# Graph network on one core: edges in four chunks, record sums beside the edge rounds, PSUM accumulation at register columns

## The chip, the cores and the metric

The kernel runs on one core of a Trainium2 chip. The time is the device time of a run in microseconds; a comparison is a median over several runs. The core has a matrix engine (PE, TensorE), a vector engine (DVE, VectorE), a scalar engine (ACT, ScalarE), GpSimd (POOL, which here issues the indirect DMAs, that is gathers and scatters with a row number per partition) and a queue engine (SP, SyncE). Each works through its own program in order and waits on semaphores for the others.

## The reference

12500 nodes with 32 features, 200000 edges sorted by destination, sources random. Everything is f32.

```python
h = relu(layernorm(x))                                   # 12500 x 32
fwd = concat(h[dst], h[src], edge_attr)                  # 200000 x 80
bwd = concat(h[src], h[dst], edge_attr)
flow = relu([fwd; bwd] @ Wf1 + bf1) @ Wf2 + bf2          # 64 wide
total = segment_sum(flow, [dst; src])                    # per node
x = x + relu(total @ Wn1 + bn1) @ Wn2 + bn2
h2 = relu(layernorm(x))
out = x + segment_sum(h2[dst], src)
```

So each edge adds a 64-wide value to its destination and another to its source, and in the second layer its destination's h2 row to its source.

## The kernel before

Nodes lie in 98 blocks of 128. Edges are worked on in tiles of 128 (one edge per partition). A tile belongs to one block of destinations, so a tile that crosses a border between blocks is worked on twice; with 1563 real tiles this makes 1664 slots, as 104 windows (NI) of 16 tiles, each window being four rounds (R) of four tiles (U). A schedule computed on the chip tells for each slot its block (`blk`), its first edge (`e0`) and its position in the ring of gathered rows (`gs_row`). It is made twice, once by destination and once by source.

**Start.** h is computed, split into three bf16 parts (`h3`), and a table `t2_rows` of 128-wide rows per node (h times the source half of Wf1) is made on PE and written to DRAM, in 26 steps. Both schedules are made.

**Edge stage.** Per round, GpSimd gathers four tiles of `t2_rows` into `ring` (L610, two rounds ahead of use) and scatters the four tiles of 67-word records of an earlier round to the place at which they lie sorted by source (L620). PE adds the gathered rows to the product of the destination's expanded features and the edge attributes (L943, L944), transposes one-hots (L914), counts how many edges of each source block came before (L955 to L959), expands destination rows (L926), and sums over destinations (L972). ScalarE evicts and applies relu (L756 to L778). VectorE computes record positions from the counts (`positions`, L1275 to L1281), adds four blocks to `acc` (L1266) and prepares the one-hots of the round after next (L1238 to L1261). SP loads source and destination numbers and the edge attributes. The scatter of a round waits for its positions and its relu.

**Record stage**, once all records have been scattered. 104 windows of 16 record slots are read back in order of source. VectorE makes one-hots u = 0 and 2 (L1337), GpSimd those of u = 1 and 3 (L654), PE multiplies each with its records into one of four banks (L1010), VectorE adds each of the four results to its block of `acc` (L1266), ScalarE copies the indices that come with the records (L802).

**Nodes.** 13 steps of the two node matrices, then the second layer norm; h2 is written to DRAM.

**Second layer.** GpSimd gathers h2 rows for each record tile (L674, 16 windows of ring), VectorE makes four one-hots per group (L1422), PE multiplies (L1072), VectorE adds four results to `xs` (L1266).

Order is as written: no scheduler moves instructions. All loops are hardware loops over windows.

Of the kernel before, what the change touches and what calls it, by code (L numbers as in the profile page):

```python
# [50 lines left out]
DA, DB, HC = 13, 8, 800  # L51
EA_PARTS = 8
H3 = 3 * D
SW = 4
TW = -(-(-(-E // P)) // W)
RING = 16
RG = 8 * W
NTW = TW
assert NI % 8 == 0 and NTW % 8 == 2 and RG >= NB - 1 + 3 * U
assert E % 125 == 0 and JC <= 512 and J % 4 == 0 and NI % SW == 0 and TW < NI - SW and EP >= TW * W * P and EP // P - W < TW * W  # L60

# [34 lines left out]
def build(nc, x, sd, ea, w12_in, w3_in, wf2e_in, wn1_in, bn1_in, wn2_in, bn2_in, out):  # L96
    with ExitStack() as ctx:
# [13 lines left out]
        by_d_sd = dram("by_d_sd", [EP, 2], I32)  # L111
        by_d_ea = dram("by_d_ea", [EA, EP])
        fb_rows = dram("fb_rows", [NP, NB])
        fb_cols = dram("fb_cols", [NP, NB])
        t2_rows = dram("t2_rows", [NBP * P, P])
        records = dram("records", [EP, REC])
# [19 lines left out]
        hprod = sb("hprod", [DA * 8, DB, 8])  # L136
        hsum = sb("hsum", [DA * 8, DB])
        hexp = sb("hexp", [DA * 8, DA, DB])
        ncol = sb("ncol", [NB, 1])
        tail_rec = sb("tail_rec", [P, REC])  # L140
        w12 = sb("w12", [P, U, P])
        w3 = sb("w3", [H3 + 1 + EA, P])
# [12 lines left out]
        ring = ring_flat.rearrange("p (t c) -> p t c", c=P)  # L155
# [3 lines left out]
        rest = ring_flat[:, 2 * LN_:RG * P]  # L159
        acc = sb("acc", [P, NBP, ACC])  # L160
        acc_flat = acc[:, :, :].rearrange("p b c -> p (b c)")
        jrow = sb("jrow", [NB, J])[:, :]

        srec = [rest[:, w * W * REC:(w + 1) * W * REC].rearrange("p (t c) -> p t c", c=REC) for w in range(SW)]
        at_ = SW * W * REC
        accs = rest[:, at_:at_ + 2 * U * ACC].rearrange("p (k u c) -> p k u c", k=2, u=U)
        at_ += 2 * U * ACC
        accT = rest[0:ACC, at_:at_ + 2 * U * P].rearrange("p (k n) -> p k n", k=2)
        at_ += 2 * U * P
        nodeT = rest[0:2 * HID, at_:at_ + U * P]  # L170
        at_ += U * P
        assert at_ <= RG * P - 2 * LN_

# [3 lines left out]
        pairs = raw[:, :, :].rearrange("p k j -> p (k j)").bitcast(F32).rearrange("p (j k) -> p j k", k=2)  # L177

        wide = sb("wide", [P, 2, J])
        wide_flat = wide[:, :, :].rearrange("p k j -> p (k j)")  # L180
# [41 lines left out]

        rec = sb("rec", [P, R, U, REC])
        rec_i = sb("rec_i", [P, R, U, 2], I32)
        sidx = sb("sidx", [P, 8, W, 2], I32)
        sdf = sb("sdf", [P, 2, U, 2])
        small = sb("small", [P, 2, 7, U])
        sblk = sb("sblk", [P, 2, U], I32)
# [1275 lines left out]
```

## Time and profile before

| | us |
|---|---|
| timed, median of 3 | 9032.03 (9025.67 to 9038.92) |
| profiled execution, first to last instruction | 7224.1 |
| start, to the first scatter | 168 |
| edge stage, to its end at | 4325 |
| record stage | 803 |
| nodes | 94 |
| second layer | 2002 |

Shares of the profiled span: PE 61%, DVE 44%, ACT 19%, GpSimd 72%. The 1808 us between the profiled span and the timed median are seen in no row of the profile. "busy" of GpSimd is the time its indirect DMAs take to issue, not the transfer. "issue" is idle time in which the engine waited for nothing that the profile shows. An f32 matmul has two records in the trace.

### The profile page before, as it was taken

What the parts mean: (1) busy time and instruction counts of PE and PEld (TensorE: products, weight loads), DVE (VectorE), ACT (ScalarE), POOL (GpSimd) and SP (SyncE); (2) the same over time, 40 slices, a digit from 0 to 9 for tenths busy, and PEclk for the clock granted to TensorE, in tenths of its full rate; (3) what the DMA queues carried; (4) which work ended last, traced back from release to release, by engine and by line L of the source; (5) the groups of instructions that cost most, each with busy time, mean ns of one, the idle gap of its engine ahead of it and who ended that gap; (6) DMA issues with size and microseconds to landing.
All of it is one profiled execution on the core that took longest, in us unless ns stands there. A gap on an engine that the chain in (4) does not pass through costs nothing.

```text
span 7224.1 us, 127054 instructions
## 1 busy us (share of the span) xinstructions
PE 4419.8 (61%) x23241; PEld 3987.8 (55%) x23244; DVE 3200.3 (44%) x15358; ACT 1352.3 (19%) x4288; POOL 5197.9 (72%) x5767
## 2 busy tenths in 40 slices
PE   4666666666666666666666679999733333333333
PEld 3655556555555655555565569999533333333333
DVE  5444444444444444444444466666523232323232
ACT  2222222222222222222222234434200000000000
POOL 2777777777777777777777766666377777777776
PEclk8666676666766666766667785555655555555555
DMA  5222222222222222222222123333111111111111
GB/s 154 43 46 43 43 43 43 43 42 43 42 43 43 42 43 42 42 42 42 43 42 42 41 35 73 71 71 73 30 14 14 14 14 14 14 14 14 14 14 20
DMA packets 1109393, 290.45 MB, mean 40 GB/s; under 512 B 992782, under 2 KB 1058701, under 8 KB 1108518
## 3 DMA queue, kind: packets, MB, share of 16 engines
q0 software_dynamic: 153824, 183.68, 10.7%
q1 hardware_dynamic: 954758, 88.54, 10.3%
q10 hardware_dynamic: 576, 16.16, 0.7%
q14 instruction: 216, 1.77, 0.1%
q8 instruction: 19, 0.31, 0.0%
HBM read 223.49 MB, written 82.32 MB: 42 GB/s over the span
## 4 chain that ended last, share of the span: by engine, by line
POOL 59%; issue 27%; DVE 6%; PE 3%; DVEq 2%; DMA 2%; POOLq 0%; ACT 0%; ACTq 0%; SPq 0%
POOL records L620 21%; POOL ring L674 20%; POOL ring L610 18%; DVE acc L1266 3%; DVEq L331 1%; PE bank L1010 1%; DVE oht L1337 1%; DVE ohd L1337 1%; DVEq L1266 1%; DMA ring<-records 0%; PE bank L943 0%; PE bank L846 0%; DMA row_next<-in_sd 0%; PE bank L944 0%; PE bank L972 0%
## 5 line engine op out<-in xcount | busy, mean ns | idle before, releaser
L620 POOL DMA_INDIRECT records<-rec,pos x1664 | 1650.3, 992 | 526.7 <-issue 507.8
L674 POOL DMA_INDIRECT ring<-h_rows,didx x1568 | 1491.1, 951 | 576.3 <-issue 477.5
L610 POOL DMA_INDIRECT ring<-t_rows,sidx x1568 | 1519.5, 969 | 484.9 <-issue 482.1
L943 PE MATMUL bank<-ring,ident 128*128 x3328 | 1094.3, 431 | 1254.6 <-DMA ring<-t_rows,sidx 1249.8
L943 PEld LDWEIGHTS bank<-ring,ident 128*128 128x128 f32 x3328 | 868.4, 320 | 1309.9 <-issue 1309.8
L1072 PE MATMUL bank<-ring,ohd 128*128 x1664 | 376.2, 402 | 1282.8 <-POOLq L684 1282.2
L1072 PEld LDWEIGHTS bank<-ring,ohd 128*128 128x128 f32 x1664 | 362.9, 330 | 1295.9 <-issue 1295.9
L1275 DVE TENSOR_TENSOR prod<-bank,q_row 128x392 f32<-128x392 f32 x416 | 235.7, 567 | 1895.8 <-PE bank L959 1895.6
L944 PE MATMUL bank<-w,cmb 113*128 113x128 f32 x3328 | 1026.2, 411 | 0.0
L1266 DVE TENSOR_TENSOR acc<-acc,bank 128x65 f32 x3328 | 734.6, 221 | 524.9 <-issue 279.1
L1266 DVE TENSOR_TENSOR xs<-xs,bank 128x32 f32 x1664 | 304.3, 183 | 1384.2 <-PE bank L1072 1371.3
L944 PEld LDWEIGHTS bank<-w,cmb 113*128 113x128 f32 x3328 | 883.0, 324 | 0.0
L773 ACT ACTIVATE rf<-bank 128x256 f32<-128x256 f32 x416 | 159.8, 384 | 2735.3 <-PE bank L944 2733.2
L972 PE MATMUL bank<-rf,ohd 128*128 128x65 f32 x3328 | 453.1, 279 | 9.7 <-ACT rec L778 0.3
L972 PEld LDWEIGHTS bank<-rf,ohd 128*128 128x128 f32 x3328 | 407.9, 193 | 54.4 <-issue 3.1
L1010 PE MATMUL bank<-ring,ohd 128*128 x1664 | 381.7, 421 | 62.4 <-POOL ohd L654 62.0
L1010 PEld LDWEIGHTS bank<-ring,ohd 128*128 128x128 f32 x1664 | 362.9, 330 | 80.7 <-issue 80.7
L802 ACT CAST raw<-ring (+1 forms) x1664 | 312.4, 192 | 478.6 <-DMA ring<-records 337.5
L1010 PE MATMUL bank<-ring,oht 128*128 x1664 | 382.3, 418 | 6.4 <-issue 6.4
L1010 PEld LDWEIGHTS bank<-ring,oht 128*128 128x128 f32 x1664 | 369.2, 332 | 10.7 <-issue 10.6
L1072 PE MATMUL bank<-ring,oht 128*128 x1664 | 374.5, 401 | 0.0
L1072 PEld LDWEIGHTS bank<-ring,oht 128*128 128x128 f32 x1664 | 367.4, 333 | 0.0
(213 smaller groups left out, 6508.9 us busy)
## 6 DMA issues: line engine op xcount, KB each, us to landing
ring<-records SPq DMA_DIRECT2D x104, 536.0 KB, 4.3
rec_i<-by_d_sd SPq DMA_DIRECT2D x1664, 1.0 KB
cmb<-by_d_ea SPq DMA_DIRECT2D x1664, 8.0 KB
records<-rec,pos POOLq DMA_INDIRECT x1664
ring<-t_rows,sidx POOLq DMA_INDIRECT x1568
ring<-h_rows,didx POOLq DMA_INDIRECT x1568, 2.4
by_d_ea<-in_ea ACTq DMA_DIRECT2D x8, 1579.0 KB, 19.1
t_rows<-cmb SPq DMA_DIRECT2D x26, 256.0 KB, 2.2
```

Source lines behind the costliest of these rows:

```text
L610: nc.gpsimd.indirect_dma_start(out=ring[:, m * W + r * U + u, :], out_offset=None, in_=t2_rows, in_offset=bass.IndirectOffsetOnAxis(ap=sid ...
L620: nc.gpsimd.indirect_dma_start(out=records, out_offset=bass.IndirectOffsetOnAxis(ap=pos[:, r, u:u + 1].bitcast(U32), axis=0), in_=rec[:, r ...
L674: nc.gpsimd.indirect_dma_start(out=h2g[:, w * W + t, :], out_offset=None, in_=h2_rows, in_offset=bass.IndirectOffsetOnAxis(ap=didx[:, k, t ...
L773: nc.scalar.activation(rf[:, :, 0:HID], pre[:, :, 0:HID], ACT.Relu)
L802: ins = nc.scalar.copy(pairs[:, bass.ds(j0 + u, 1), :].rearrange("p a k -> p (a k)"), srec[w][:, bass.ds(at[u], 1), HID + 1:REC].bitcast(I ...
L943: nc.tensor.matmul(p, ident[:, :], ring[:, bass.ds(at[u], 1), :].rearrange("p a c -> p (a c)"), start=True, stop=False)
L944: ins = nc.tensor.matmul(p, cmb[:, r, u, :], w3[:, :], start=False, stop=True)
L972: ins = nc.tensor.matmul(pb[3][:, u * ACC:(u + 1) * ACC], ohd[:, r % 2, u, :], rf[:, u, :], start=True, stop=True)
L1010: ins = nc.tensor.matmul(s_bank[r][:, u * ACC:(u + 1) * ACC], s_oh[r][:, u, :], srec[w][:, bass.ds(at[r * U + u], 1), 0:ACC].rearrange("p ...
L1072: ins = nc.tensor.matmul(s_bank[r][:, u * D:(u + 1) * D], s_oh[r][:, u, :], h2g[:, bass.ds(at[r * U + u], 1), :].rearrange("p a f -> p (a ...
L1266: return nc.vector.tensor_tensor(to, to, src[:, u * width:(u + 1) * width], ALU.add)
L1275: placed = chain.link(nc.vector.tensor_tensor(prod[:, :, :], q[:, 0:U, :], bcast_mid(q_row[:, r % 2, :], U), ALU.add))
```

## The change

1. **Edges and records in chunks.** The edge tiles are divided into four chunks of 480, 400, 336 and 347 tiles. Records are sorted by source within their chunk. A chunk's records are complete once its edges are through, so they can be summed while the next chunk's edges are worked on. Record windows are now of 24 slots (`SWIN`), six groups (`SG`) of four; there are 84 of them (`NS`), 2016 slots instead of 1664. The record position's base per chunk comes in through one more matmul in `counts` (a row of offsets chosen by a register).
2. **Sums beside the edges.** From edge window 40 (`I0`) on, each edge window also sums one record window: two groups in rounds 0 and 2, one in rounds 1 and 3 (`PLAN`). PE does `sum_records`, VectorE `sum_step`, which adds a group's four results one by one and makes all four one-hots of the group after; ScalarE keeps two index columns per window for the second layer (`keep_columns`). GpSimd makes no one-hots any more. 64 windows are summed so.
3. **The other 20 windows** (120 groups) come after the edges, in `add_up_records`: a one-row matmul clears 260 columns, the four products are accumulated at columns that depend on the slot's block (same block as its predecessor or the next), and VectorE adds all four blocks in one instruction of 260 columns.
4. **The second layer** sums in the same way, 504 groups with one add of 128 columns each; its gathers are written out without a loop and take their indices from the kept columns.
5. **Gathers of the edge stage** fetch 96 bf16 numbers (the three parts of h) instead of 128 f32 numbers; the table steps at the start are gone. PE transposes the gathered rows (`transpose_sources`), ScalarE evicts them, and the product with the source weights joins the one with the attributes. A product with the destination weights takes the place of the product with the identity. Gathers lead by four rounds (`LEAD`), and scatters stand ahead of gathers.
6. **Source and destination numbers** are loaded once into SBUF; ScalarE picks them per tile (`pick_edges`) instead of four loads per round on SP.
7. The **source schedule** is made after the first edge window instead of before it.

```diff
+PLAN = (2, 1, 2, 1)
+CHUNKS = (480, 400, 336, -(-E // P) - 1216)
+SR = 2
+I0 = 40
...
-            def gather_t2(s, m, r):
+            def gather_h3(s, m, r):
...
+            def sum_records(s, m):
+
+                n = s * SG + m
+                at = four(pe, slot_row, n * U, SR * SWIN - 1)
+                pe.wait_ge(soh_ready, n + 1)
+                pe.sem_inc(pe_tick, 1)
+                for u in range(U):
+                    ins = nc.tensor.matmul(e_bank[m % 2][:, u * ACC:(u + 1) * ACC], e_oh[m % 2][:, u, :],
+                                           srec[:, bass.ds(at[u], 1), 0:ACC].rearrange("p a c -> p (a c)"), start=True, stop=True)
+                ins.then_inc(ssum_ready, 1)
+
+            def add_up_records(s, m):
...
+                nc.tensor.matmul(e_bank[m % 2][:, 0:U * ACC], ones_h[0:1, :], before_h[0:1, 0:1].broadcast_to([1, U * ACC]), start=True, stop=False)
+                for u in range(U):
+                    ins = nc.tensor.matmul(e_bank[m % 2][:, block_columns(to, u, ACC)], e_oh[m % 2][:, u, :],
+                                           srec[:, bass.ds(at[u], 1), 0:ACC].rearrange("p a c -> p (a c)"), start=False, stop=u == U - 1)
+                ins.then_inc(ssum_ready, 1)
...
+            def sum_step(s, m, adds=True, ahead=True, behind=None):
...
+                for u in range(U):
+                    if adds:
+                        dve.wait_ge(dve_s, DS0 + (n - 1) * U + u)
+                        ins = add_step(acc, at, e_bank[(m - 1) % 2], ACC, u)
+                        ins.then_inc(dve_s, 1)
+                    if ahead:
+                        record_one_hot(s1, m1, at1, u)
...
+                    m = sum(PLAN[:r + 1]) - 1
+                    if s is not None and PLAN[r] == 2:
+                        sum_step(s, m - 1, adds=not (start and m == 1), behind=i * R + r)
+                    add_and_prepare(i, r, first, ahead, None if s is None or start and r == 0 else (s * SG + m - 1) * U)
+                    if s is not None:
+                        sum_step(s, m, behind=i * R + r + 1)
```

VectorE, from the end of a round's positions to its first add to `acc`. Before (`TENSOR_LOAD sched` reads the blocks of four slots into registers, `ISA` is a wait or a register step):

```order
L1280 TENSOR_REDUCE small<-prod 128x4
L1281 TENSOR_TENSOR pos<-small 128x4
L325 TENSOR_LOAD sched
L1266 ISA
L1266 TENSOR_TENSOR acc<-acc,bank 128x65
L1238 CAST sdf<-rec_i 128x8
```

After, in a round with two record groups:

```order
L1388 TENSOR_TENSOR pos<-small 128x4
L364 ISA
L364 TENSOR_LOAD sched
L364 ISA
L364 TENSOR_LOAD sched
L1454 REGISTER_ALU
L1373 ISA
L1373 TENSOR_TENSOR acc<-acc,bank 128x65
L1432 ISA
L1432 REGISTER_ALU
L1432 TENSOR_SCALAR oht<-iota,wide,ring 128x128
L1454 REGISTER_ALU
```

Two register loads and four pairs of add and one-hot have come between the positions and the edges' own adds; the same stands once more behind those adds.

TensorE, between the counts and the sums of a round. Before (`sched` is the destination block, `h` is `h3`):

```order
L959 MATMUL bank<-ohs,ones_h 128x98
L325 ISA
L325 TENSOR_LOAD sched
L926 ISA
L926 MATMUL bank<-oht,h 96x128
```

After, in a round with two record groups (`ring` is the records' ring, the one-hots lie in `ring` or `oht`):

```order
L979 MATMUL bank<-ohs,ones_h 128x98
L364 ISA
L364 TENSOR_LOAD sched
L999 REGISTER_ALU
L1002 ISA
L1002 MATMUL bank<-ring 128x65
L1002 ISA
L1002 MATMUL bank<-ring 128x65
```

A group's four matmuls stand ahead of the expansion; the second group's stand behind the round's sums (L992), ahead of the next round's hidden layer.

GpSimd, in the loop over windows. Before:

```order
L610 DMA ring<-t_rows,sidx 128x128 x4
L615 ISA
L620 DMA records<-rec,pos 202112x67 x4
L610 DMA ring<-t_rows,sidx 128x128 x4
L615 REGISTER_ALU
```

After:

```order
L662 DMA records<-rec,pos 212352x67 x4
L649 REGISTER_ALU
L652 DMA ring<-h_rows,sidx 128x96 x4
L657 REGISTER_ALU
L662 DMA records<-rec,pos 212352x67 x4
```

As many indirect DMAs per round as before, the scatters now first and the gathers two rounds further ahead.

## Rows read from the trace of the kernel before

**Rows 1.** The page: span, and the chain that ended last by engine.

```profile
span 7224.1 us, 127054 instructions
...
POOL 59%; issue 27%; DVE 6%; PE 3%; DVEq 2%; DMA 2%; POOLq 0%; ACT 0%; ACTq 0%; SPq 0%
```

**Rows 2.** Windows by stage: length, busy us (count) by engine, PEclk, DMA share, GB/s.

```profile
160.00:4180.00 4020.00, 2709.66 (x14921) 2358.56 (x14920) 1820.41 (x8625) 923.41 (x2355) 3065.50 (x3129) 0.69 0.22 43
4180.00:4325.00 145.00, 116.76 (x881) 101.59 (x878) 106.37 (x502) 54.36 (x139) 95.97 (x98) 0.91 0.13 25
4325.00:5128.00 803.00, 742.06 (x3329) 719.42 (x3329) 515.17 (x2595) 312.36 (x1664) 516.15 (x936) 0.50 0.35 71
...
5222.00:7224.00 2002.00, 730.65 (x3328) 717.54 (x3328) 610.85 (x3316) 0.00 (x0) 1491.08 (x1568) 0.50 0.15 15
```

**Rows 3.** The page's costliest groups: count, busy us, mean ns, idle before by releaser.

```profile
L620 POOL DMA_INDIRECT records<-rec,pos x1664 | 1650.3, 992 | 526.7 <-issue 507.8
L674 POOL DMA_INDIRECT ring<-h_rows,didx x1568 | 1491.1, 951 | 576.3 <-issue 477.5
```

**Rows 4.** Timeline of GpSimd: the first scatter of two rounds (start us, us).

```profile
1503.38 1.01 POOL L620 DMA_INDIRECT records<-rec,pos  x1 [0.30 <-issue]
...
1513.64 1.01 POOL L620 DMA_INDIRECT records<-rec,pos  x1 [0.30 <-issue]
```

**Rows 5.** Timeline of VectorE: a round with gathers, and two rounds without.

```profile
1510.72 0.57 DVE L1275 TENSOR_TENSOR prod<-bank,q_row 128x392 f32<-128x392 f32 x1 [4.88 <-PE bank L959]
...
1513.31 0.22 DVE L1266 TENSOR_TENSOR acc<-acc,bank 128x65 f32 x1 [0.58 <-issue]
...
4187.35 0.57 DVE L1275 TENSOR_TENSOR prod<-bank,q_row 128x392 f32<-128x392 f32 x1 [1.60 <-PE bank L959]
...
4192.64 0.56 DVE L1275 TENSOR_TENSOR prod<-bank,q_row 128x392 f32<-128x392 f32 x1
```

**Rows 6.** Timeline of TensorE: hidden layer from its start to the next work, twice.

```profile
1505.34 0.79 PE L943 MATMUL bank<-ring,ident 128*128 x2 [3.27 <-DMA ring<-t_rows,sidx]
...
1508.91 0.63 PE L914 MATMUL bank<-ident_h,ohd_h 128*128 128x128 bf16 x4
...
166.17 0.48 PE L943 MATMUL bank<-ring,ident 128*128 x2 [0.17 <-issue]
...
168.32 0.38 PE L914 MATMUL bank<-ident_h,ohd_h 128*128 128x128 bf16 x4
```

**Rows 7.** Timeline of TensorE in the record stage: four groups, then the next.

```profile
4379.29 3.67 PE L1010 MATMUL bank<-ring,ohd 128*128 x16 [0.42 <-POOL ohd L654]
4382.76 3.62 PE L1010 MATMUL bank<-ring,oht 128*128 x16
4386.94 3.67 PE L1010 MATMUL bank<-ring,ohd 128*128 x16 [0.56 <-POOL ohd L654]
```

**Rows 8.** The page's groups: VectorE's adds of 65 and of 32 columns.

```profile
L1266 DVE TENSOR_TENSOR acc<-acc,bank 128x65 f32 x3328 | 734.6, 221 | 524.9 <-issue 279.1
L1266 DVE TENSOR_TENSOR xs<-xs,bank 128x32 f32 x1664 | 304.3, 183 | 1384.2 <-PE bank L1072 1371.3
```

**Rows 9.** Timeline of VectorE in the second layer: two adds with a one-hot between.

```profile
6300.67 0.18 DVE L1266 TENSOR_TENSOR xs<-xs,bank 128x32 f32 x1
...
6301.00 0.18 DVE L1266 TENSOR_TENSOR xs<-xs,bank 128x32 f32 x1
```

**Rows 10.** Timeline of GpSimd: the first scatter.

```profile
167.62 1.04 POOL L620 DMA_INDIRECT records<-rec,pos  x1 [0.30 <-issue]
```

**Rows 11.** The chain of waits: what follows the last gather.

```profile
7190.52 4.72 DMA ring<-h_rows,didx
...
7195.77 13.87 PE bank L1072 x64
```

**Rows 12.** Groups of instructions from 1000 to 2000 us, shapes apart: two of ScalarE's.

```profile
L762 ACT ACTIVATE cmb<-bank 96x512 f32<-96x512 f32 x97 | 57.6, 593 | 104.0 <-PE bank L926 98.7 <-issue 5.2
...
L777 ACT COPY rec<-rec_i 128x8 int32<-128x8 int32 x97 | 18.6, 192 | 0.0
```

More of the change, by code:

```diff
@@ L327, in four, with block_columns @@
                 skip_runtime_bounds_check_because="the schedule clamps it to this range")[1]
[L329 to L333 removed]
+        def block_columns(at, u, width):
+            if u == 0:
+                return slice(0, width)
+            step = nc.s_assert_within(at[u] - at[0], 0, u, skip_runtime_bounds_check_because="a slot's block is its predecessor's or the next one")
+            return bass.ds(step * width, width)
         def rounds(eng, body):
@@ L447, in _ @@
             sp.wait_ge(h2_written, 16)
-            for k in range(2):
-                sp.wait_ge(t2_written[k], 16 * (NG // 2))
+            sp.wait_ge(h3_written, 16)
         FB_STEPS = 15
@@ new lines, in slack_of @@
+            def slack_of(n_chunks, scale):
+                first, last, over, tiles = (tile_col[:, m, 0:n_chunks] for m in range(4))
+                own.step(nc.vector.tensor_tensor(slack[:, 0:n_chunks], last, first, ALU.subtract))
+                own.step(nc.vector.tensor_tensor(slack[:, 0:n_chunks], slack[:, 0:n_chunks], tiles, ALU.subtract))
+                own.link(nc.vector.tensor_scalar(slack_h[:, 0:n_chunks], slack[:, 0:n_chunks], scale, None, ALU.mult))
+            dve.wait_ge(n_ready, 1)
@@ new lines, in planned @@
+            def planned(q):
+                vals = nc.values_load_multi_w_load_instructions(
+                    tail_plan[0:1, bass.ds(q * PLANNED, PLANNED)], engines=[dve.engine], min_val=0, max_val=NB,
+                    skip_runtime_bounds_check_because="the schedule clamps it to this range")[1]
+                slots = [nc.s_assert_within(v, 0, SR * SWIN - 1, skip_runtime_bounds_check_because="a slot's tile is one of the two windows loaded") for v in vals[0:2 * U]]
+                return slots, vals[2 * U:PLANNED]
@@ L1304, in _, with tail_pairs, edges @@
+            def tail_pairs(s, last):
+                for k in range(SG // 2 - last):
+                    slots, blocks = planned((s - TAIL) * (SG // 2) + k)
+                    tail_step(s, 2 * k + 1, blocks[0], slots[0:U])
+                    s1, m1 = (s, 2 * k + 2) if k < SG // 2 - 1 else (s + 1, 0)
+                    tail_step(s1, m1, blocks[1], slots[U:2 * U])
             assert U == 4
             per = R * (8 + 3 + 3)
-            def edges(i, first, last):
+            def edges(i, first, last, s=None, start=False):
```

1076 lines of the change are left out of this document (586 added, 490 removed).

## Prediction, made before the changed kernel was run

> **What bounds the kernel now.** The profiled execution spans 7224.1 us; the three timed runs have a median of 9032 us. The chain that ended last is 59% GpSimd and 27% issue [rows 1]: start from GpSimd. Cut by stage [rows 2], the span is 4165 us of edges (160 to 4325), 803 us in which the records are summed by source, 94 us of node networks, and 2002 us of the second layer. In the edge stage GpSimd is 76% busy by the trace and has no other wait than "issue" [rows 2, 3], that is, it issues one indirect DMA behind the other. One round (four gathers, four scatters) starts 10.26 us after the last [rows 4]. The second layer is 1568 gathers of 951 ns plus 0.30 us of issue, 1.255 us each [rows 3], again without a wait. In the record stage GpSimd issues no DMA: TensorE is 92% busy at a granted clock of 0.50 (1.2 GHz) and a group of four tiles takes 7.65/4 = 1.91 us [rows 7]. So: two stages bound by the number of indirect DMAs, which the change leaves alone (1664 + 1568 + 1568), and between them 803 us bound by TensorE.
>
> **How the timed runs stand to the trace.** 1808 us of the median are not in the profiled span. If they belong to the 4800 indirect DMAs (0.38 us each) or to something fixed, they stay as they are; if every duration is longer by 9032/7224 = 1.25, what is saved counts 1.25 times. I carry both and take a value between.
>
> **Part 1, start of the edges.** The 26 table steps go; the source schedule and its chain of small VectorE steps move behind the first window, where GpSimd has its 16 leading gathers and the first scatters to issue. Against it stand a load of the tiles, a histogram in four parts and, while VectorE makes the source schedule, a wait of GpSimd for positions. The first scatter now starts at 167.6 us [rows 10]. I take -10 us, bounds -30 and +30.
>
> **Part 2, windows 0 to 39.** The gathers fetch 192-byte rows instead of 512-byte ones; the second layer's rows of 128 bytes take 951 ns, the scatters 992 [rows 3], so size hardly matters. VectorE idles 4.88 us of each round waiting for TensorE, TensorE 3.27 us waiting for a gather [rows 5, 6]. Into that goes, on ScalarE, one more eviction of 593 ns and four picks of 192 ns each [rows 12], some 1.4 us in the loop between TensorE and ScalarE, and on TensorE four bf16 transposes and one more count matmul. The loop by itself takes 5.29 us when no gather holds it (from 4187.35 to 4192.64) [rows 5]; with 1.4 and a register load or two it is 7 to 8 us, under 10.26. Cost: 0. The cover that makes it 0 is GpSimd's round.
>
> **Part 3, windows 40 to 103 (256 rounds).** Each window also sums six groups, 1.5 per round. *VectorE:* an add and a one-hot follow each other in 0.33 us in the second layer [rows 9]; the add here has 65 columns, 221 instead of 183 ns [rows 8], so 0.37 us, four of them 1.5 us. Two register loads stand before them; one costs 0.58 us [rows 5]. So 2.6 us per group and 3.9 per round, on 5.29: **9.2 us of 10.26**. *TensorE:* four f32 matmuls per group are 1.72 us at 1.2 GHz (eight, with two records each, in 3.47) [rows 7] and half at 2.4; the eight of the hidden layer take 3.57 us at the one level and 2.15 at the other [rows 6]. Per round: 6.9 us busy now (67%), plus 1.3 to 2.6, plus some 0.5 to 0.9 for transposes and counts: 8.7 to 10.4. *Together:* in rounds with two groups TensorE can start the second only after VectorE's positions (2.0 us) and one group step (2.6 us); then it has 0.9 to 1.7 us of sums, 2.15 to 3.57 of hidden and 1.2 to 2.0 of transposes and counts before VectorE can go on: 8.9 to 11.9 us. Rounds with one group are shorter, VectorE 7.9 us. GpSimd can absorb the swing: the gathers lead by four rounds instead of two. The mean is thus between 10.26 and about 11; I take 10.6. For the 228 rounds with gathers (160 to 387): 228 x 0.34 = **+78 us**.
>
> **Part 4, the last rounds.** Without gathers the rounds now take 5.3 us in a row [rows 5] and 5.4 in the mean, because neither GpSimd (four scatters, 5.1 us) nor VectorE asks for more. With the sums in them VectorE alone needs 9.2. Before: 26 rounds x 5.4 and 2 more x 10.26 = 161 us; after: 28 rounds x 10.2 = 286. **+125 us.** The last windows are where the moved work is not free.
>
> **Part 5, the record stage.** 803 us go. What comes: the last 20 of 84 windows, 120 groups, 4 x 0.43 us of matmul [rows 7] and a one-row matmul that clears 260 columns, about 0.25 us; VectorE makes four one-hots and one wide add, some 1.6 us beside it. I take 2.1 us per group (bounds 1.9 and 2.6), 252 us and 8 us to drain the last scatters and load: 260. **-543 us.**
>
> **Part 6, the rest.** Nodes: unchanged, 94 us. Second layer: the same 1568 gathers; 504 groups instead of 416, of 1.72 + 0.2 us on TensorE in 1968/504 = 3.9 us: hidden. After the last gather came 4.7 us of DMA and 13.9 us of matmuls [rows 11]; now windows of 24 slots wait for it, one or two, 12 us each: +10 us.
>
> **Sum.** -10 + 78 + 125 - 543 + 10 = **-340 us**, a span of 6884. With the 1808 us kept: 8692. With everything times 1.25: 8607. If the extra time is in the indirect DMAs, their round is long enough (13.3 us) to hide all of part 3, and part 4 shrinks to about 28 x 9.8 - 26 x 6.6 = 100 less 2 x 13.3: -10 + 0 + 76 - 543 + 10 = -467, that is 8565. I forecast **8630 us**, 4.5% less.
>
> **Rivals.**
> (a) *VectorE and TensorE wait for each other* and the round settles at 11.9, the upper end above, in half of the rounds: mean 11.3. Then 256 x 0.7 = +180 us on the forecast: 8810. For it: both engines run their queue in order and each needs the other twice per round; against it: a granted clock of 0.91 where the rounds follow closely [rows 2], 0.69 where TensorE idles. Chance 0.19.
> (b) *GpSimd itself slows.* An indirect DMA has 951 ns where VectorE is 31% busy and, as a scatter, 992 where it is 45% busy [rows 2, 3]. Continued to about 80%, that is some 0.08 us more, x 8 x 228 = +146 us: 8776. The Trainium skill ("SBUF — State Buffer", Who interferes with whom) says that a DMA issued from GpSimd cannot write its descriptors while a VectorE copy or tensor_scalar runs in a two-port mode, and the added one-hots are tensor_scalars with SBUF operands. By that rule GpSimd would be held here; the rows show at most 40 ns of it. Chance 0.10.
> (c) *Slower than before.* The change stops paying when 256 rounds lose another 340 us, at 10.6 + 1.33 = 11.9 us per round. The mechanism: TensorE stays at 1.2 GHz (as in the record stage, 0.50 at 92% busy [rows 2]), every round takes the long path of 11.9 us and its three extra register loads (0.58 each, half exposed) add 0.9: 12.8 us. Then 256 x 2.2 = +563: 9190 us. It decides from 11.9 on. Against it: the edge stage has 0.69 already, and 0.91 where its rounds follow closely. Chance 0.07.
> (d) *The extra time of the timed runs hides part 3 completely, or scales it*: 8540 us. Chance 0.12.
> The forecast itself keeps 0.52. That the change does not do what it says is no case of weight: the counts of instructions are fixed by the program.
>
> The Trainium skill ("TensorE: Matmul & The Clock Gate", What's actually happening) says that TensorE's default is half clock and that activity releases it. The edge stage's 0.69 at 67% busy against 0.91 in its last rounds agrees [rows 2], the record stage (0.50 at 92%) does not. By the rule part 3 would come out at the lower TensorE figures and the sum would be 78 us better.
>
> **Numbers.** Leaving out (c), and the best corner of (d), the range is 8480 to 8880. Differences under 0.2% (18 us) can't be told from none. Faster by more: the forecast, (a), (b) and (d) hold 0.93, of which 0.01 goes to mixtures that end near no change: 0.92; within: 0.01; slower: (c), 0.07.
>
> **What would show each step right or wrong.** In the trace of after: scatters of two rounds 10.3 to 10.8 us apart in windows 40 to 97 (part 3), with GpSimd's idle put down to "issue"; if it is put down to VectorE's positions, (a) or (c) holds, and VectorE's wait for the counts says which engine leads. Indirect DMAs over 1.03 us in the mean would be (b). 28 rounds of about 10 us after the last gather (part 4). A stage of about 260 us with 260-column adds, 2.1 us apart (part 5). The span near 6884 us; and the difference of timed median and span either still near 1808 or 1.25 times. I am wrong above all if the round in the windows with sums is set by VectorE and TensorE at over 11 us.

## The result: 3.8% slower, and the profile after

| | us |
|---|---|
| before, median of 4 | 9033.23 (9025.67 to 9038.92) |
| after, median of 4 | 9374.38 (9370.51 to 9388.35) |
| ratio | 1.0382 [1.0367, 1.0397] |
| profiled execution of after, first to last instruction | 9386.8 |

The span of after is its time, 9387 us. The gap of 1808 us that the profile of before showed was no part of the kernel: the same kernel takes 7221 or 7225 us on two of the chips of the runs below (1 and 9) and 9012 to 9110 us on four others (0, 11, 12, 14). No chip was seen as both, and chip 11 was tried twice (9109 and 9017 us). I call the first kind **chip A** and the second **chip B**; whether the chip itself makes the difference or something around it is not shown. By its span, the profile shown ahead of the prediction is of chip A; by their times, both kernels were timed on chip B. Run e0_before is before, unchanged, on chip B, with a span of 9025.0 us and a time of 9026.65. So the two can be compared stage by stage, from the starts of their scatters and gathers, one profiled execution each (a second profile of after, run e15_after_again, has each stage within 12 us of these):

| stage | before, chip B | after, chip B | difference | forecast |
|---|---|---|---|---|
| to the first scatter | 169.7 | 160.9 | -9 | -10 |
| windows 0 to 39 | 2190 | 2233 | +43 | 0 |
| windows 40 to 96 (228 rounds) | 3129 | 3498 | **+370** | +78 |
| windows 97 to 103 | 236 | 327 | +90 | +125 |
| from the last scatter to the first h2 gather | 901 | 438 | -463 | -543 |
| the 1568 gathers of h2 | 2273 | 2528 | **+254** | 0 |
| after the last gather | 126 | 202 | **+77** | +10 |
| sum | 9025 | 9387 | +362 | -340 |

The page of after: span, busy times, clock, and the rows that answer to [rows 1, 3]:

```profile
span 9386.8 us, 143672 instructions
PE 5464.5 (58%) x27143; PEld 4722.2 (50%) x27144; DVE 3703.0 (39%) x15684; ACT 1471.8 (16%) x4905; POOL 4688.7 (50%) x4832
...
PEclk8565555555666666666666666655655555555555
...
another core or an unknown queue 43%; PE 22%; issue 18%; ACT 6%; DVE 5%; DVEq 5%; ACTq 2%; DMA 1%; POOL 0%; SPq 0%; POOLq 0%
...
L662 POOL DMA_INDIRECT records<-rec,pos x1664 | 1660.4, 998 | 2459.7 <-DVE pos L1388 1856.1
L694 POOL DMA_INDIRECT ring<-h_rows,ring x1568 | 1495.6, 954 | 1470.3 <-issue 453.1
...
L1382 DVE TENSOR_TENSOR prod<-bank,q_row 128x392 f32<-128x392 f32 x416 | 235.1, 565 | 1684.5 <-remote 1514.8
```

GpSimd is 50% busy, not 72%, and is 0% of the chain. Its indirect DMAs are as long as before (998 and 954 ns); what has grown is the waiting ahead of them, 1856 us of it for VectorE's positions, and VectorE in turn waits at its counts for something that the profile can't name ("another core or an unknown queue", "remote" in the rows). That already holds for before on chip B (run e0_before, the same rows):

```profile
span 9025.0 us, 127056 instructions
...
L620 POOL DMA_INDIRECT records<-rec,pos x1664 | 1649.0, 991 | 1914.4 <-DVE pos L1281 1430.5
...
L1275 DVE TENSOR_TENSOR prod<-bank,q_row 128x392 f32<-128x392 f32 x416 | 235.7, 567 | 2072.4 <-remote 1908.9
```

**What holds them.** The timeline of e0_before, one round: GpSimd issues four scatters and four gathers in a row. TensorE's last count matmul (L959) ends at 995.81. VectorE, which waits for nothing else then, starts its positions at 1002.15, 1.50 us after GpSimd's last gather ended (999.70 + 0.95):

```profile
990.68 1.01 POOL L620 DMA_INDIRECT records<-rec,pos  x1 [4.50 <-DVE pos L1281]
...
994.58 0.98 POOL L620 DMA_INDIRECT records<-rec,pos  x1 [0.30 <-issue]
...
995.39 0.42 PE L959 MATMUL bank<-ohs,ones_h 128*128 128x294 bf16 x3
...
995.86 1.00 POOL L610 DMA_INDIRECT ring<-t_rows,sidx  x1 [0.30 <-issue]
...
997.83 0.60 ACT L756 ACTIVATE oht<-bank 128x512 bf16<-128x512 bf16 x1 [2.15 <-remote]
...
999.70 0.95 POOL L610 DMA_INDIRECT ring<-t_rows,sidx  x1 [0.30 <-issue]
...
1002.15 0.57 DVE L1275 TENSOR_TENSOR prod<-bank,q_row 128x392 f32<-128x392 f32 x1 [7.89 <-remote]
...
1005.12 1.01 POOL L620 DMA_INDIRECT records<-rec,pos  x1 [4.47 <-DVE pos L1281]
```

On chip A the same two instructions follow each other at once. In the trace of before, in the midst of GpSimd's issuing:

```profile
996.14 0.42 PE L959 MATMUL bank<-ohs,ones_h 128*128 128x294 bf16 x3
...
996.60 0.57 DVE L1275 TENSOR_TENSOR prod<-bank,q_row 128x392 f32<-128x392 f32 x1 [4.74 <-PE bank L959]
```

Between 700 and 2200 us this takes 0.04 us there in every round; in e0_before it takes 5.1 us in the median. So in a typical round on chip B there are 10.3 us of issuing, then 1.3 to 1.5 us until TensorE's signal arrives, then 2 us of positions. It is not so in every round: ScalarE's row at 997.83 starts while GpSimd issues (TensorE's transposes for it had ended at 995.05), and in three of ten rounds of that stretch the positions do too. By its place in the window (windows 40 to 96) a round takes 14.3, 10.9, 15.2 and 14.6 us, 13.7 in the mean instead of 10.27. GpSimd's round thus covers much less than on chip A, because most of the signals come in its breaks. Where no indirect DMA is issued, nothing is held: the stage from the last scatter to the first h2 gather takes 901 us on chip B and 900 on chip A. The 1801 us between the chips lie in the edge stage (1400) and the second layer (398).

### The profile page after: what moved, and what is told of

It reads as the page before. It is cut to its first block, busy times and chain, and to the rows that moved or that the text cites. A ratio compares the mean times of both kernels' runs of the same rounds, so it can differ in the third digit from the quotient of the medians.

```text
span 9386.8 us, 143672 instructions
## 1 busy us (share of the span) xinstructions
PE 5464.5 (58%) x27143; PEld 4722.2 (50%) x27144; DVE 3703.0 (39%) x15684; ACT 1471.8 (16%) x4905; POOL 4688.7 (50%) x4832
## 4 chain that ended last, share of the span: by engine, by line
another core or an unknown queue 43%; PE 22%; issue 18%; ACT 6%; DVE 5%; DVEq 5%; ACTq 2%; DMA 1%; POOL 0%; SPq 0%; POOLq 0%
PE bank L1115 7%; PE bank L992 5%; PE bank L959 2%; PE bank L960 2%; ACT oht L746 2%; DVEq L364 2%; PE bank L935 2%; PE bank L1015 1%; ACTq L364 1%; ACT rec_i L777 1%; ACT cmb L752 1%; DVE oht L1583 1%; DVE ohd L1583 1%; DVEq L1416 1%
## 5 line engine op out<-in xcount | busy, mean ns | idle before, releaser
L694 POOL DMA_INDIRECT ring<-h_rows,ring x1568 | 1495.6, 954 | 1470.3 <-issue 453.1
L652 POOL DMA_INDIRECT ring<-h_rows,sidx x1568 | 1522.2, 971 | 513.6 <-issue 477.5
L959 PE MATMUL bank<-wdst,ring 96*128 96x128 f32 x3328 | 1085.0, 429 | 461.5 <-ACT ring L755 442.1
L959 PEld LDWEIGHTS bank<-wdst,ring 96*128 96x128 f32 x3328 | 889.7, 327 | 477.3 <-issue 477.2
L960 PE MATMUL bank<-wsrc,cmb 113*128 113x128 f32 x3328 | 1031.3, 412 | 0.0
L935 PE MATMUL bank<-oht,h 128*96 128x128 bf16 x1664 | 283.0, 311 | 1073.6 <-ACT oht L746 1022.7
L960 PEld LDWEIGHTS bank<-wsrc,cmb 113*128 113x128 f32 x3328 | 890.8, 327 | 0.0
L992 PE MATMUL bank<-rf,ohd 128*128 128x65 f32 x3328 | 758.4, 402 | 2.8
L992 PEld LDWEIGHTS bank<-rf,ohd 128*128 128x128 f32 x3328 | 698.7, 310 | 39.7 <-issue 2.9
L1115 PE MATMUL bank<-ring,oht 128*128 x2016 | 502.3, 403 | 160.9 <-issue 156.3
L1115 PEld LDWEIGHTS bank<-ring,oht 128*128 128x128 f32 x2016 | 457.4, 325 | 206.5 <-issue 178.0
```

Source lines behind the costliest of these rows:

```text
L652: nc.gpsimd.indirect_dma_start(out=hring[:, m * W + r * U + u, :], out_offset=None, in_=h3_rows, in_offset=bass.IndirectOffsetOnAxis(ap=si ...
L694: nc.gpsimd.indirect_dma_start(out=h2g[:, t % (RING * W), :], out_offset=None, in_=h2_rows, in_offset=bass.IndirectOffsetOnAxis(ap=dst_til ...
L935: ins = nc.tensor.matmul(pb[1][0:H3, u * P:(u + 1) * P], h3[:, bass.ds(at[u], 1), :].rearrange("p a c -> p (a c)"), oht_h[:, r % 2, u, :], ...
L959: nc.tensor.matmul(p, cmb_dst[:, r % 2, u, :], wdst[:, :], start=True, stop=False)
L960: ins = nc.tensor.matmul(p, cmb[:, r, u, :], wsrc[:, :], start=False, stop=True)
L992: ins = nc.tensor.matmul(pb[3][:, u * ACC:(u + 1) * ACC], ohd[:, r % 2, u, :], rf[:, u, :], start=True, stop=True)
```

## Experiments

### Is it GpSimd's issuing? (e0, e1, e2, e10, e11)

> The kernel before, unchanged, to see where the 1808 us between its profiled span (7224.1 us) and its timed median (9033) belong; the changed kernel has no such gap (span 9386.8, time 9388.4). Theory 1 (the profile shown was not the state in which the kernel is timed): span within 2 us of its time, near 9030 us, and the extra time visible in rows: the round of the edge stage at about 10.26 x 1.25 = 12.8 us instead of 10.26. Theory 2 (something outside the span): span 7224 again with a time of 9030. Under theory 1 the wait of VectorE for TensorE's counts, 7 to 9 us in the changed kernel, should be seen here as well, and matmuls whose semaphores come microseconds after their rows end.

Measured: 9026.65 us, span 9025.0, round 13.72 us in the mean. Theory 1 holds; the rows are above.

e1_after_pause, between a round's scatters and gathers (and in e2_before_pause the same line, for `+ 1`, in the kernel before):

```diff
                         if m2 < gathers:
+                            pool.wait_ge(q_ready, (s * 8 + m) * R + r + 2)
+                            pool.sem_inc(pool_tick, 1)
                             gather_h3(s + m2 // 8, m2 % 8, r2)
```

> The changed kernel with one wait more: GpSimd waits, between a round's four scatters and the four gathers behind them, for TensorE's counts of the next round. Theory 1 (while GpSimd issues indirect DMAs back to back, TensorE's signals reach the others only after a break; the round is 10.3 us of issuing, then 1.5 us until the signals come, then 2 us of positions): the counts come in the new break and the positions are made beside the gathers; the round falls from 13.8 to about 12 us without sums and from 15.3 to about 13.5 with them, 388 rounds x 1.75, so about 8700 us. Theory 2 (the time between VectorE's steps belongs to TensorE and ScalarE themselves, and GpSimd only waits for it): the wait adds its 1.5 us to each of 388 rounds, about 9950 us.

> The kernel before with the same wait: GpSimd waits for TensorE's counts of round v before it issues the gathers for round v + 2 and then the scatters of v. Theory 1: the round falls from 13.7 to about 12 us, 388 x 1.7, about 8370 us. Theory 2: 1.5 us more per round, about 9600 us.

Measured: e1 **9006.8 us** (after: 9374), e2 **8595.24 us** beside 9012.63 of before. A wait added to every round makes both kernels 4 to 5% faster on chip B (one run each), so theory 2 falls. The gain is under theory 1's, 8700 and 8370 us: the round falls to 12.41 us without sums and 12.60 in the kernel before, not to 12; with sums to 14.65, so the gain there is 0.7 and not 1.8 us. The timeline of e1, GpSimd and the positions: the counts' row ends at 1002.42, before the last two scatters are issued, and is seen 1.26 us after the last one ended (1004.70 + 0.98).

```profile
1002.00 0.42 PE L981 MATMUL bank<-ohs,ones_h 128*128 128x294 bf16 x3
...
1004.70 0.98 POOL L662 DMA_INDIRECT records<-rec,pos  x1 [0.30 <-issue]
1006.94 0.57 DVE L1384 TENSOR_TENSOR prod<-bank,q_row 128x392 f32<-128x392 f32 x1 [7.14 <-remote]
...
1007.75 1.26 POOL L652 DMA_INDIRECT ring<-h_rows,sidx  x1 [2.07 <-remote]
...
1013.30 1.01 POOL L662 DMA_INDIRECT records<-rec,pos  x1 [0.30 <-issue]
```

The positions now lie beside the gathers, and the next scatter follows the last gather without a wait.

Two more edits of the kernel before make the break without TensorE: other work on GpSimd, or the landing of its own scatters.

```diff
+                nc.gpsimd.tensor_scalar(spare[:, 0:448], spare[:, 0:448], 1.0, None, ALU.is_equal).then_inc(idled, 1)
...
+                                pool.wait_ge(sct[(r - 1) % R], 16 * U * (s * 8 + m - (r == 0) + 1))
+                                pool.sem_inc(pool_tick, 1)
```

> The kernel before with one GpSimd instruction more per round, ahead of its gathers: a tensor_scalar on a tile of its own, 128x448, some 2.1 us by the 0.61 us of its 128x128 ones. It waits for nobody. Theory 1 (the issuing of indirect DMAs is what holds the signals, and any break in it frees them): the round falls from 13.7 to about 12.6 us, as with the wait of run e2_before_pause: 8600 us within 80. Theory 3 (any work of GpSimd holds them): 388 x 2.1 us more, about 9850 us.

> The kernel before with a wait of GpSimd for the landing of the scatters just issued, ahead of the gathers, in place of the wait for TensorE's counts. Theory 1: a break of some 2 us, whatever it waits for, frees the signals: round 12.6 us, 8600 us within 80. If only a wait tied to TensorE's signal helps, the break adds 2 us to each of 388 rounds, about 9800 us.

Measured, beside 9109.44 us of before on that chip: e10 **8685.13** (ratio 0.953), e11 **8545.15** (0.938). A break in which GpSimd is busy with something else frees the signals too:

```profile
1009.86 0.98 POOL L631 DMA_INDIRECT records<-rec,pos  x1 [0.30 <-issue]
1010.86 1.38 POOL L614 TENSOR_SCALAR spare<-spare 128x448 f32<-128x448 f32 x1
1012.41 1.04 POOL L621 DMA_INDIRECT ring<-t_rows,sidx  x1 [0.17 <-issue]
```

(1.38 us instead of the 2.1 expected; the round is 12.73 us.) So what holds goes with the issuing of indirect DMAs, not with GpSimd's work, and a missing dependency isn't it. Whether it is the issuing itself or what follows from it, such as the transfers and the reports of their landing, no run separates.

### The sums beside the edges (e3, e6, e8, e12, e13, e16, e17, e7)

e3_sums_late has `I0 = 84` for `I0 = 40`.

> The changed kernel with the sums beside the edges started at window 84 instead of 40: 44 windows (264 groups) go from beside the edges into the stage behind them. If the sums are what lengthens the round from 13.8 to 15.3 us, windows 40 to 83 are back at 13.8 (176 x 1.5 = -270 us) and the stage behind grows by 264 x 2.8 us = +739: about 9845 us. If the sums cost nothing beside the edges and something else in the later windows is slow (the first 44 rows of the index columns, the clock), the whole 739 us come on top: about 10110 us.

Measured: 9839.74 us, as expected if the sums lengthen the round. (The changed kernel was not timed in this batch or in the next; the kernel before differs by up to 1% between batches, so the rounds say more than the totals.) The round of windows 40 to 83 is back at 13.75 us, with sums it is 15.34. The moved work costs 1.57 us per round or 6.3 us per window beside the edges; behind them it costs 16.9, since e3 takes 465 us more than after for 44 windows, 10.6 each, on top of the 6.3.

e6_wide_adds (e8_wide_adds_pause is this with the wait of e1):

```diff
-                        sum_records(s, sum(PLAN[:r]))
+                        add_up_records(s, sum(PLAN[:r]))
...
-                        ins = add_step(acc, at, e_bank[(m - 1) % 2], ACC, u)
+                    add_blocks(at, e_bank[(m - 1) % 2]).then_inc(dve_s, 1)
```

> The changed kernel with the record groups beside the edges summed as those behind them are: TensorE clears 260 columns and accumulates at columns from registers, VectorE adds once per group instead of four times. If VectorE's string of small steps (four adds with their registers, 0.5 us apart, and longer while GpSimd issues) is what lengthens the round by 1.6 us, three adds of four go: 1.5 groups x 1.4 us = 2 us less on VectorE per round, so the round is back near 14.2 us and the kernel at 9376 - 256 x 1.1 = about 9090 us. If it is TensorE's part (it now has 0.37 us of clearing and a 0.5 us register load more per group): 256 x 1.3 = +330, about 9700 us.

> Run e6_wide_adds with the wait of run e1_after_pause. If both gains are independent: e6_wide_adds less about 370 us, near 8720 us if e6_wide_adds comes out at 9090. If VectorE's string was hidden once the signals come earlier, it equals e1_after_pause, 9007 us.

Measured: e6 **9262.03**, e8 **8711.39**. The round with sums is 14.89 in e6 (from 15.32) and 13.46 in e8. Both edits trade three of VectorE's adds per group for a clearing and a register load on TensorE. Net of these the wide add is worth 0.43 of the 1.55 us, much less than the 1.1 expected; with the signals freed earlier it is worth 1.2 us (14.65 to 13.46).

For the rest, one of four one-hots (e12) and one of four matmuls (e13) per group were kept. What is left out is as the expectations say.

```diff
-                    if ahead:
+                    if ahead and (u == U - 1 or isinstance(s, int)):
...
-                for u in range(U):
+                for u in range(1):
```

> The changed kernel with one of four one-hots per record group beside the edges made (the other three are left out, so these sums are not the reference's). If VectorE's string sets the round with sums, 3 x 0.34 us and the register steps around them go, some 1.4 us per group and 2 us per round: the round falls from 15.3 to about 14.0 us and the kernel by 256 x 1.3 to about 9040 us. If TensorE's matmuls set it: no change, 9376 us within 50.

> The changed kernel with one of four matmuls per record group beside the edges (the other three are left out). If TensorE sets the round with sums, 3 x 0.4 us per group, 1.8 us per round, go: the counts are done earlier, the round falls to about 14.0 us and the kernel to about 9040 us. If VectorE's string sets it: no change, 9376 us within 50.

Both ran on chip A, where the kernel before takes 7221.31 us (7216.38 to 7223.73): e12 **7316.98**, e13 **7243.83**. Repeated, because the split was wanted for chip B, they fell on a chip A again: e16 7303.83 and e17 7252.18, before 7224.51.

> Run e12_one_hot_each once more. On a chip with held signals (before near 9030 us): if VectorE's string sets the round with sums, it falls from 15.3 to 14.0 us, the kernel to about 9040 us; if TensorE's matmuls set it, 9376 us within 50. On a chip without them: 7317 us again.

> Run e13_one_matmul once more. On a chip with held signals: if TensorE sets the round with sums, it falls from 15.3 to 14.0 us, the kernel to about 9040 us; if VectorE's string does, 9376 us within 50. On a chip without them: 7244 us again.

So the split on chip B stays open. But the runs say something else: **even where nothing is held, and with part of the added work left out, the change is no gain**, but 1.3% (e12), 1.1% (e16), 0.3% (e13) and 0.4% (e17) slower, each from one run beside executions of before of 7216 to 7225 us. By stages, e12 against the profile ahead of the prediction: start -15 us, windows 0 to 39 +29 us (10.30 for 10.27 us per round), windows 40 to 96 **+373** (11.92 for 10.28), the last windows +152, record stage -463, gathers -6, after them +21. One round with two groups in e12's timeline (TensorE, VectorE, GpSimd):

```profile
3006.03 0.57 DVE L1382 TENSOR_TENSOR prod<-bank,q_row 128x392 f32<-128x392 f32 x1 [3.07 <-issue]
...
3007.87 0.16 DVE L1388 TENSOR_TENSOR pos<-small 128x4 int32<-128x4 f32 x1
3008.99 1.01 POOL L662 DMA_INDIRECT records<-rec,pos  x1 [2.29 <-DVE pos L1388]
...
3011.81 1.96 PE L1002 MATMUL bank<-ring,oht 128*128 x8 [4.42 <-DVE oht L1432]
```

The waits of the same run from 1900 to 4500 us (windows 42 to 96; us in total, times, longest):

```profile
POOL records L662 <- DVE pos L1388: 364.3, 150, 3.9
PE bank L1002 <- DVE oht L1432: 309.1, 103, 5.8
...
PE bank L1002 <- DVE ring L1432: 172.0, 105, 3.5
```

TensorE works in order. Its `sum_records` stands ahead of the expansion and hidden layer of the next round, and there it waits 4.42 us for one-hots that VectorE makes only after its positions and adds (481 us in all). By the order of the engines' programs that wait passes to the next counts, to the positions, and to GpSimd, whose 364 us of waiting for positions are about what the rounds of this stretch have grown by. Neither engine's added work sets the round alone: with three matmuls of four away it is still 11.63 us, with three one-hots of four away 11.92. The chain of e12 from 1900 to 4400 us goes back and forth between the two; in it VectorE's register loads (0.56 us each, four per round) have 11.1% and TensorE's record sums 7.7%. So the waiting is shown, and that it outweighs the work is argued: no run took the waiting away and left the work.

e7_old_order puts the gathers ahead of the scatters again, with `LEAD = 2`.

> The changed kernel with the order of the kernel before on GpSimd: gathers ahead of the scatters and two rounds ahead instead of four. Nothing waits for a gather in the changed kernel's rounds, and the kernel before has the same mean round in its windows 0 to 39 (13.72 against 13.77 us) with this order: no change, 9376 us within 40. If the order is part of the loss in the windows with sums, the time falls by over 100 us.

Measured: 9328.91 us, 0.5% or 47 us less, from one run, where 40 were allowed; rounds 13.65 and 15.17 (13.77 and 15.34 in after). That is less than what the kernel before differs by between batches: little or nothing hangs on the order.

### The second layer (e4, e9, e5, e14)

e4_quarter_gathers2, a quarter of the gathers of h2:

```diff
-                for t in range(w * W, w * W + W):
+                for t in range(w * W, w * W + W, 4):
...
-                    pool.wait_ge(gh[(w - 1) % SW], 16 * W * ((w - 1) // SW + 1))
+                    pool.wait_ge(gh[(w - 1) % SW], 4 * W * ((w - 1) // SW + 1))
```

> The changed kernel with only every fourth gather of the second layer issued (392 of 1568; the other rows are left out, and what is summed in their place is stale). Theory 1 (TensorE and VectorE are held while GpSimd issues, else they need 3 us per group of four slots, as at the chunks' ends in the changed kernel's trace): the second layer falls from 2730 to about 504 x 3.0 = 1510 us, the kernel to about 8170, and the register steps of 0.7 us on TensorE are gone. Theory 2 (the groups need 4.6 us by themselves): 504 x 4.6 = 2320 us, about 8970.

Measured: 8276.3 us; the second layer takes 1626 us instead of 2730, 3.2 us per group. The second layer's matmuls in after, by their line, 6720 to 6900 us; the first row is the register step ahead of them (ns: shortest, median, longest):

```profile
L1115 PEldq FUSED_REGOPS  x63: 5/700/1397, 6726.4 to 6888.1; - x63
...
L1115 PE MATMUL bank<-ring,oht x40: 390/401/415, 6724.4 to 6886.3; 128*128 x40
...
L1115 PE MATMUL bank<-ring,ohd x32: 389/398/403, 6761.5 to 6868.1; 128*128 x32
```

The same line and stretch in e4:

```profile
L1115 PEldq FUSED_REGOPS  x378: 3/100/709, 6729.8 to 6897.9; - x189
...
L1115 PE MATMUL bank<-ring,oht x224: 393/401/418, 6727.8 to 6898.5; 128*128 x112
...
L1115 PE MATMUL bank<-ring,ohd x208: 401/401/418, 6741.4 to 6892.7; 128*128 x104
```

While GpSimd issues without a break (after), a register step on TensorE takes 700 ns, and 72 matmuls are recorded in the stretch in which e4 has 432. None are missing from the record: over the whole layer both traces hold 4032, eight per group. The matmuls themselves are as long. The slow register steps go with the lag but don't make it: e0_before does one group per 20 us too (also 72 matmuls, 6700 to 6900 us), and its register steps are short:

```profile
L1072 PEldq FUSED_REGOPS  x36: 55/55/55, 6717.2 to 6896.1; - x36
```

So TensorE falls behind, by one group done per window of 16 gathers, until the ring of gathered rows is full. From window 16 on, GpSimd has to wait once in each window: 2.9 us, in which the signals pass and four groups get done. That makes 22.9 us per window instead of 20.0. The change has 88 groups more, since every chunk crosses all borders between blocks once more, and GpSimd's rule (`slots_done`) asks for 30 to 34 groups at once where a chunk ends, at 2.6 to 2.7 us each:

```profile
7720.32 0.94 POOL L694 DMA_INDIRECT ring<-h_rows,ring  x1 [3.21 <-remote]
...
7832.80 0.94 POOL L694 DMA_INDIRECT ring<-h_rows,ring  x1 [92.78 <-PE bank L1115]
```

Three such steps (windows 45, 70, 91) take 112.5, 97.7 and 111.8 us instead of 22.9: 253 us, the whole +254. The fourth chunk's end is in the +77.

e9_smooth_ring asks for at most six groups per window, and keeps GpSimd near TensorE:

```diff
-                if w >= RING:
-                    pool.wait_ge(nsum_ready, slots_done(w - RING))
+                sure = SG * sum(t < W * (w - 1) for t, _ in ends)
+                due = max(min(sure - 2 * SG, due + 6), slots_done(w - RING) if w >= RING else 0, 0)
+                if due > 0:
+                    pool.wait_ge(nsum_ready, due)
```

> Run e8_wide_adds_pause with another rule for GpSimd's waits in the second layer: it is kept two record windows behind what TensorE can surely have done, and the 30 groups that its old rule asks for at once at the end of a chunk (stalls of 65 to 90 us at windows 15, 45, 70 and 91) are spread at up to six groups per window. Theory 1 (signals pass in breaks, and a short break passes several groups, 4 in 2.8 us, while a long one passes one per 3 us): the three stalls of 253 us shrink to about 90, the first stall goes, the lag at the end falls from 202 to about 100 us: 8711 - 160 - 30 - 100 = about 8420 us. Theory 2 (a group costs its 3 us wherever it stands): about 8680 us.

Measured: 8776.82 us, 0.9638 [0.9622, 0.9654] of before; e8 was 8711.39, or 0.964 of the 9034 beside it. No gain: **theory 1 fell here.** The second layer, from its first gather to the end, takes 2713 us, 2719 in e8. The stalls are gone, but windows with six groups take 27.9 us, where those with four took 22.9 in e8: 2.5 us per group more. Spreading the groups doesn't hide them.

e5_before_near is e2 with GpSimd within three windows of TensorE in the second layer (`NEAR = 3`):

```diff
-                    if not first:
-                        pool.wait_ge(nsum_ready, R * (i * RING + w - RING + behind))
+                    if not first or w > NEAR:
+                        pool.wait_ge(nsum_ready, R * (i * RING + w - NEAR))
```

> The kernel before with the wait of run e2_before_pause and, in the second layer, GpSimd kept within three windows of TensorE instead of eight. Theory 1 (signals come only in breaks, so TensorE falls behind until GpSimd has to wait for it; the first stall, 56 us at window 15, and the 126 us after the last gather are that lag): the windows stay at 23.2 us, the stall at window 15 goes and the end shrinks to about 50 us, against some 3 us more in each of the first 12 windows: 8595 - 56 - 70 + 36 = about 8500 us. Theory 2 (the windows' time is TensorE's own, and the early breaks are lost): about 8600 us or more.

Measured: 8542.52 us, 0.9456 [0.9429, 0.9483] of before: 53 us under e2, which ran on another chip B. The gathers take 33 us less, the stall at window 15 less what the early windows lost; the end shrank from 114 to 88 us, not to 50.

e14_landing_near joins e11 and e5, and ran on chip A:

> The kernel before with the wait of run e11_before_landing (GpSimd waits for the landing of its scatters ahead of the gathers) and with GpSimd kept within three windows of TensorE in the second layer, as in e5_before_near. If both gains are independent: e11_before_landing was 0.938 of the kernel before, e5_before_near 55 us under e2_before_pause, together 0.932, some 8420 us where the kernel before takes 9034.

Measured: 7998.38 us, **1.1077** [1.1062, 1.1092] of before. The breaks that save 6% on chip B cost 777 us on chip A: 388 waits of 2.0 us, with nothing to free. Its round is 12.29 us against 10.28. None of the kernels that ran on chip A (e12, e13, e14, e16, e17) beat the one before there.

### The change once more (e15)

> The changed kernel, unchanged, once more, beside the kernel before. If the chip is one on which the kernel before takes 7221 us, two theories: (1) only the held signals made the change lose, so it gains here: a round with sums near 10.6 us and about 6900 us; (2) the round with sums is long by its own string of steps (e12_one_hot_each and e13_one_matmul, with part of it left out, still took 11.9 and 11.6 us per round here): 12.3 us, and 7316 + 256 x 0.4 = about 7420 us, 2.7% slower than before. If the chip is one of the others: 9376 us within 1%, against 9030 to 9110.

Measured, on a chip B: 9373.58 us, 1.0397 [1.0367, 1.0427]. The changed kernel as it is did not run on chip A; that it is slower there too is argued from e12, e13, e16 and e17, which do less work and were all 0.3 to 1.3% slower than before, and not shown.

## Why the prediction was wrong, step by step

**The timed runs and the trace.** The step failed first: the 1808 us were carried along, kept or scaled, as if they had no place. They lie only where indirect DMAs are issued, and not in the DMAs' own duration (991 ns) but in waits around them. Both of my readings (0.38 us more for each of the 4800, or everything times 1.25) leave GpSimd as the bound; it no longer was one. The profile whose span was not the time was of another kind of chip, and its covers did not hold.

**Part 1 (-10).** -9. Right. **Part 2 (0).** The round is as before on both chips (13.77 for 13.72, 10.30 for 10.27). Right, though on chip B for another reason: the round is set there by the held signals, which the change leaves as they are. Missed were 43 us, mostly in window 0, where the source schedule is made.

**Part 3 (+78).** This step failed on both chips: +370 (1.62 us per round where 0.34 was forecast) and, with part of the work left out, +373. I gave VectorE 9.2 us of work and TensorE 8.7 to 10.4, wrote 8.9 to 11.9 for both together, and took 10.6, because GpSimd could absorb the swing. The upper end was the one to take: the engines meet twice per round, and with two groups in it TensorE stands at `sum_records`. That is rival (a) in its mechanism. Its price had the round of 11.9 us in half of the rounds only; on chip A all rounds together average 11.9, with less work. On chip B the sums add 1.55 us to 13.77 (windows 40 to 83); how that splits between the held signals and the two engines' waiting stays open, but for the 0.43 us of the wide add.

**Part 4 (+125).** +90; on chip A, with part left out, +152. Right in direction and near in size. **Part 5 (-543).** -463: the term that was mis-sized is the group behind the edges, 2.72 us and not 2.1. TensorE in after's timeline:

```profile
6403.52 0.37 PE L1013 MATMUL bank<-before_h,ones_h 1*128 1x260 bf16 x1 [0.46 <-issue]
...
6403.82 1.97 PE L1015 MATMUL bank<-ring 128*128 x8
...
6406.23 0.37 PE L1013 MATMUL bank<-before_h,ones_h 1*128 1x260 bf16 x1 [0.45 <-issue]
```

The matmuls take 1.97 us, not 1.72, the clearing 0.37, not 0.25, and 0.45 is two register loads and their wait, not counted; over 120 groups that is 74 of the 80 us missed. **Part 6 (+10).** This failed on chip B: +331. "504 groups in 3.9 us each: hidden" took the cover from a trace in which TensorE had kept pace; on chip A it is hidden indeed (-6 and +21).

**The rivals.** (c), slower, came true with a chance of 0.07. Its round of 12.8 us lies above the 11.9 of e12 on chip A and under the 15.3 of chip B, but its mechanism, TensorE at half clock, wasn't the cause: the granted clock of windows 40 to 96 is 0.62 in after and 0.62 in e0_before (chip A: 0.71 in e12, 0.69 in before). (b), GpSimd slowed by VectorE, did not happen: 998 and 971 ns with the sums beside them, 992 and 969 before [rows 3]. The rule of the Trainium skill cited there ("SBUF — State Buffer", Who interferes with whom) has a VectorE instruction hold up a DMA of GpSimd; what was found on chip B is another thing, other engines' signals held up while GpSimd issues. By the rule of the Trainium skill on the clock ("TensorE: Matmul & The Clock Gate", What's actually happening) part 3 would have come out lower; that was not seen either: the stage grew by 370 us, not by less than 78. No rival had the second layer in it. The range ended at 8880, 490 us under the result.

## What to carry to other kernels

Ahead of any sum, see that the profiled span is the timed time; where it isn't, the work that covers an added step may not exist in the timed runs. Before work is put beside a loop of two engines that wait for each other, look where it stands in the order of the engine that runs ahead: if it waits for the other one there, it lengthens the round by the wait, not by its own time. And count work in groups, borders included: four chunks made 504 groups of 416.

## What the runs showed of the hardware

On chip B, signals of TensorE reach VectorE and ScalarE late while GpSimd issues indirect DMAs every 1.25 to 1.3 us: 5.1 us in the median from the counts to the positions (e0_before), most often 1.3 to 1.5 us after the last DMA ended. On chip A it is 0.04 us with the same program. In the second layer of after on chip B, register steps of TensorE take 700 or 1400 ns, where e4 with a quarter of the gathers has 100 in the median. A break of 1.4 us per eight DMAs brings 424 us and one of some 2 us 564 us, beside the same runs of before (e10, e11).

What the two kinds of chip differ in is open. One hint: the trace of e0_before on chip B holds 59344 semaphore updates, that of the same program on chip A 155291, and all 14 traces of chip B hold 42000 to 60000, all 6 of chip A over 131000. The instructions are all there (127056 and 127054), so on chip B it is records of semaphores that are missing. That is probably also why the profile calls the releaser "remote". The Trainium skill ("NOTIFIC — the notification-queue block", Overflow: three behaviours, one of which stalls the engine) says that the block's inner pipeline holds its producers back rather than lose a record inside. That would fit engines that slow down while many DMAs report their landing, but it is a guess, and it doesn't say where the missing records went. Every time in this document, of both kinds of chip, is of an execution for which span and clock were recorded; no run has the records off. So it stays untested whether chip B would be slower than chip A, and whether the breaks would help it, when nothing is recorded.
